# Attention stage: the nine expert parts of two tiles added by four whole additions, in place of one sum along the parts for each tile

## The reference

```
y1  = layernorm(x + attention(x))                    # 4 heads of 32, over 16 sequences at one position
idx = argmax(softmax(y1 @ wg)); gate = the largest probability     # 8 experts, each token goes to one
y   = ((y1 @ w1[idx] + b1[idx]) @ w2[idx] + b2[idx]) # 128 -> 512 -> 128, nothing nonlinear between
out = layernorm(y1 + (gate * y if the token found room at its expert else 0))
```

## Time and profile before

| | |
|---|---|
| median of 3 runs | 4655.11 us (4639.43 to 4656.45) |
| the profiled execution's own time | 4655.05 us |
| its span, first to last instruction | 4653.3 us |
| mean granted TensorE clock | 0.897 |
| busy over the span: PE, DVE, ACT, POOL | 83%, 67%, 37%, 34% |
| attention stage, first to last reduce of the experts | 4083.1 to 4534.6 us |

### The profile page before, as it was taken

How to read it: one execution, slowest core, us unless ns; L and a number is a source line. 1 busy time by engine, 2 the same in 40 slices (tenths; PEclk the granted TensorE clock), 3 DMA queues, 4 the chain that set the end, 5 groups by cost and what they waited for, 6 DMA issues and landing times. The chain is left out here.

```text
span 4653.3 us, 163745 instructions
## 1 busy us (share of the span) xinstructions
PE 3861.4 (83%) x66245; PEld 2812.4 (60%) x66245; DVE 3117.4 (67%) x6104; ACT 1733.8 (37%) x3495; POOL 1595.7 (34%) x2519
## 2 busy tenths in 40 slices
PE   6999999866648998989988989989899998588860
PEld 4666666533326776767776767767677766455530
DVE  3777777747746676767666766767677654288858
ACT  1222222224423343444443433434444432277750
POOL 1333333311004454444444444544444443100001
PEclk6998999988858999999999999999999987699975
DMA  0222222136522222222222222222222221111105
GB/s 25 44 47 46 55 56 49 42 84 155 158 65 49 42 56 41 47 51 48 50 47 49 48 49 40 57 42 47 51 48 49 49 47 26 55 27 28 28 18 149
DMA packets 695281, 251.77 MB, mean 54 GB/s; under 512 B 529368, under 2 KB 660128, under 8 KB 694176
## 3 DMA queue, kind: packets, MB, share of 16 engines
q1 hardware_dynamic: 694560, 241.62, 23.7%
HBM read 154.63 MB, written 86.79 MB: 52 GB/s over the span
## 5 line engine op out<-in xcount | busy, mean ns | idle before, releaser
L1373 POOL TENSOR_TENSOR d_f<-d_ms,d_mhalf 128x16 f32<-128x16 f32 x64 | 239.5, 3742 | 965.1 <-DVE d_ms L1807 965.1
L1567 PE MATMUL d_pa<-d_wv,d_hs 128*128 128x512 f32 x1024 | 517.6, 652 | 0.9 <-DVE d_qk L1778 0.4
L1761 DVE SCALAR_TENSOR_TENSOR d_acc<-d_pa,d_cq,d_acc 128x512 f32<-128x512 f32 x576 | 431.7, 750 | 95.2 <-ACT d_acc L1406 80.3
L1383 POOL TENSOR_TENSOR d_prod<-d_ablk,d_tblk 128x15 f32<-128x15 f32 (+7 forms) x960 | 342.5, 357 | 218.5 <-DMA d_ablk<-a_blocks 147.9
L1387 POOL TENSOR_TENSOR d_tblk<-d_tblk,d_prod 128x28 f32<-128x28 f32 (+7 forms) x896 | 336.4, 375 | 70.8 <-POOL d_prod L1383 0.2
L1567 PEld LDWEIGHTS d_pa<-d_wv,d_hs 128*128 128x128 f32 x1024 | 219.5, 215 | 232.1 <-issue 220.2
L1542 PE MATMUL d_pa<-d_hq,d_wqk 128*128 128x259 f32 x768 | 255.4, 462 | 81.4 <-DVE d_acc L1761 58.0
L1406 ACT ACTIVATE d_acc<-d_pa,d_cq 128x512 f32<-128x512 f32 x192 | 131.9, 687 | 420.8 <-PE d_pa L1542 418.0
L262 POOL TENSOR_TENSOR a_act<-a_act,a_cws 128x512 f32<-128x512 f32 x128 | 166.8, 1316 | 310.2 <-DMA a_cws<-cw_rows 165.3
L1580 PEld LDWEIGHTS d_pb<-d_of_head,d_sqT 128*128 128x128 f32 x2048 | 246.2, 196 | 39.2 <-issue 39.0
L1370 POOL TENSOR_TENSOR d_nr<-d_n,d_half_power 128x16 f32<-128x16 f32 x64 | 188.0, 2938 | 193.8 <-DVE d_n L1846 179.8
(11 more groups left out here) (371 smaller groups left out, 9418.3 us busy)
## 6 DMA issues: line engine op xcount, KB each, us to landing
a_cws<-cw_rows SPq DMA_DIRECT2D x32, 1024.0 KB, 10.5
decays<-g_dec SPq DMA_DIRECT2D x16, 2048.0 KB, 7.3
d_dd<-decays SPq DMA_DIRECT2D x64, 512.0 KB, 4.3
d_hs<-h_t SPq DMA_DIRECT2D x512, 32.0 KB, 2.2
t_blocks<-d_tblk SPq DMA_DIRECT2D x128, 128.0 KB, 1.7
a_blocks<-d_at SPq DMA_DIRECT2D x512, 16.0 KB, 1.9
d_ablk<-a_blocks SPq DMA_DIRECT2D x64, 128.0 KB, 2.1
d_tt<-t_blocks SPq DMA_DIRECT2D x512, 16.0 KB
```

Source lines behind the costliest of these rows:

```text
L1373: pool.tensor_tensor(f[:, :], ms[:, :], mhalf[:, :], ALU.pow).then_inc(sem("f_ready"), 1)
L1383: link(pool.tensor_tensor(prod[:, 0:n, 0:s + 1], ablk[:, s, s + 1:SB].unsqueeze(2).to_broadcast([P, n, s + 1]), tblk[:, 0, s, 0:s + 1].uns ...
L1567: last = pe.matmul(pa[:, B + m, :], hs[:, u % 2, t, :], wv[:, t, cols(m)], start=(t == 0), stop=(t == TAPS - 1))
L1761: last = dve.scalar_tensor_tensor(out=own, in0=raw(e)[:, :, t:t + QT], scalar=cq[:, t, col:col + 1], in1=own, op0=ALU.mult, op1=ALU.add)
```

## The change

`reduce(c)`, called four times in an iteration, becomes `reduce(pair)`, called twice. It takes two tiles by four additions: parts 0 to 3 plus parts 4 to 7 (1024 numbers in each partition), of these the first two plus the second two (512), the first plus the bias part (256), and the last two into `moe` (256). The first three write back into `part`, and each has a `link`. The first pair stands where `reduce(1)` stood, and the second where `reduce(3)` stood. Those who wait for `reduced` count two in an iteration instead of four, and the loop counts 50 links instead of 38.

```diff
@@ sync and scalar: SP before it stores moe, ACT before weigh(0)
-                    hold(sem("reduced"), NC * (i - 1))
+                    hold(sem("reduced"), 2 * (i - 1))
...
-                    wait(act, sem("reduced"), NC * (i - 2))
+                    wait(act, sem("reduced"), 2 * (i - 2))
@@ vector
-                def reduce(c):
+                def reduce(pair):
                     if not main:
                         return
-                    if c == 0:
+                    these = slice(2 * pair, 2 * pair + 2)
+                    if pair == 0:
                         wait(dve, sem("moe_stored"), 16 * NC * (i - 2))
                         dve.wait_ge(sem("bias_taken"), i - 1)
-                    dve.wait_ge(sem("weighed"), HALVES * (i - 2) + 2 * c + 2)
-                    dve.tensor_reduce(moe[:, c, :], part[:, c, :, :].rearrange("p e d -> p d e"), AX_X, ALU.add)\
+                    dve.wait_ge(sem("weighed"), HALVES * (i - 2) + 4 * pair + 4)
+                    link(dve.tensor_tensor(part[:, these, 0:4, :], part[:, these, 0:4, :], part[:, these, 4:8, :], ALU.add))
+                    link(dve.tensor_tensor(part[:, these, 0:2, :], part[:, these, 0:2, :], part[:, these, 2:4, :], ALU.add))
+                    link(dve.tensor_tensor(part[:, these, 0, :], part[:, these, 0, :], part[:, these, NE, :], ALU.add))
+                    dve.tensor_tensor(moe[:, these, :], part[:, these, 0, :], part[:, these, 1, :], ALU.add)\
                        .then_inc(sem("reduced"), 1)
...
-                reduce(0)                    # was behind the sums of the layernorm of y
...
-                reduce(1)
+                reduce(0)                    # behind the sums of the next x
...
-                reduce(2)                    # was behind rden
...
-                reduce(3)
+                reduce(1)                    # ahead of v
```

More of the change, by code:

```diff
@@ L1920, in attention_phase @@
     LOOP_FIRST, LOOP_LAST = 2, 6
-    DVE_LINKS = 38
+    DVE_LINKS = 50
     with ExitStack() as ctx:
```

## The result

| | before | changed |
|---|---|---|
| median of 20 runs each, us | 4640.99 (4629.76 to 4660.17) | 4658.59 (4635.73 to 4672.94) |
| ratio, 95% interval | | 1.0033 [1.0019, 1.0048] |
| profiled execution, us | 4655.05 | 4661.11 |

A forecast was written before the change was run, and what follows sets the result against it. The prediction took a path through `rt`, ACT and PE, not DVE, to bound the attention stage. Delays of 5.2, 0.8, 0.3 and 0.8 us made 7.1 us on 4655.05, forecast 4662 us, range 4641 to 4677.

The forecast's parts named there:

- What bounds the stage: Attention stage: from `rt` to the logits the path is PE and ACT alone, though DVE is busiest at 86%.
- the ring: One attention iteration, 28.5 us: `rt` on DVE, ACT and PE work to the logits, `lm`, routing chain, next `rt`.
- The prices of the additions: The four additions of a pair take 1.22, 0.69, 0.42 and 0.42 us; DVE's busy time falls 48 us.
- The first pair hidden: Additions for tiles 0 and 1, behind the sums of x: hidden by waits for PE, cost and gain nothing.
- The second pair: Additions for tiles 2 and 3 behind the last `weigh`: `lm` 3.40 us after their start instead of 2.97, 0.43 later.
- The sum, 7.1 us: Delay over all iterations: 12 x 0.43 = 5.2 us, plus 0.8, 0.3 and 0.8 in iterations 15, 16 and 17.
- iteration 4's 0.70 us wait of `v`: First iteration in the loop: `v` had waited 0.70 us for PE, which takes the whole delay, so 0.
- its allowance for dearer additions: Upper bound 4677 us: an extra 1.0 us, one held-up addition, in each of 15 iterations.
- a DVE bound: Rival, 5%: DVE sets the pace of the attention stage; 2.7 us saved an iteration, 43 us in all, 4612 us.
- The free tail: Rival, 15%: the 0.43 us ahead of `lm` is swallowed; only the last iterations' 1.9 us stay, 4657 us.
- Additions held up by POOL: Rival, 5%: two additions behind the last `weigh` held up 0.95 us each, 28 us more in 15 iterations, 4690 us.

The follow-up runs named there:

- first pair only: Kernel before with tiles 0 and 1 added by four additions, tiles 2 and 3 still summed where they were: ratio 1.0011 [0.9992, 1.0030].
- last tile alone: Changed kernel with tile 2 added earlier, behind `rden`, and only tile 3 added ahead of `v`: ratio to the kernel before 1.0003 [0.9985, 1.0020].

## Why the prediction was right, and where it was short

- *What bounds the stage*: right. Not the busiest engine, but the ring over `rt`, ACT and PE; taking 1.3 and 2.2 us of each iteration off DVE gained nothing (first pair only, last tile alone).
- *The prices of the additions*: 1.23, 0.69, 0.43, 0.43 against 1.22, 0.69, 0.42, 0.42, and 49 us less of DVE's work against 48. The rows that the prices came from are products of the same sizes (L1868, L523); the additions took the same within 0.02 us.
- *The first pair hidden*: right. `h` is in time and `on` waits for PE, 3.3 us in iteration 4 where 3 were expected.
- *The second pair*: right to 0.01 us, 3.39 against 3.40, and 28.85 in an iteration against 28.9.
- *The sum, 7.1 us*: this step was too small, less than half of the 15 us measured. As the ring's own share it nearly holds: 5.6 us over iterations 2 to 14 against 5.2; behind them stand 4.0 against 1.9, with a lower clock in that stretch too (0.82 and 0.73 in the last two iterations against 0.99 and 0.61). What is missing is that the granted clock would change with the ring's length: 17.7 us of the stage in the profiled execution. I took iteration 4's 0.70 us wait of `v` for the start of the loop; it was a fall of the clock (the mean granted clock of that iteration is 0.85), the only one there, and its 33.11 us against 28.42 said what another one costs. The sum put the clock at nothing without a reason. That the median, 4658.59, came so near to 4662 is luck: the 7.1 us stood on a median of three runs that lay 14 us above that of twenty, and on 4641 they give 4648, 10.5 too low. As a ratio, 1.0015 was forecast and 1.0033 measured; the range reached so far by its allowance for dearer additions, 1.0 us in each iteration, which did not come.
- *The rivals*: a DVE bound was refuted, and came true only where three copies more were put on DVE. The free tail was refuted. Additions held up by POOL: not seen, here not even in the first pair, which was to stretch by 1.0 us; in six of thirteen iterations it was POOL that waited, below.

## What to carry to other kernels

Look for what the wait in front of an instruction leaves behind it: batching two tiles halves the instructions but puts both tiles' work behind the last one's arrival, so batch what is early and keep alone what comes last. Time saved on an engine off the ring is worth nothing until work of the ring is moved onto it; here three copies turned it into 0.5%, where the same copies on the kernel with the sums gave 0.26%. And where PE works in bursts, price a longer ring also by the granted clock, iteration by iteration.

## What was not expected of the hardware

- A delay of 0.43 us in each iteration of 28.4 raised the falls of TensorE's clock to 1.2 GHz from one to four whole ones (4.3 us each) and three or four part ones (1.4 us), alike in three kernels, one execution each; 1.04 us gave a part fall in every iteration but the first, and iterations of 27.0 to 28.1 us had no whole one. Before the fall shown above PE had worked in bursts, 1.0 to 1.4 of each 2 us, but it did the same in iterations without a fall. What picks the iteration is open.
- The first pair's first addition and POOL's power of 1.01 us start within 0.2 us of each other. By the exclusion that the earlier trace rows show and the Trainium skill states ("SBUF — State Buffer", section "Who interferes with whom"), one of the two should wait for the other. Which one does, and whether, hangs here on which came first. In iteration 6 POOL was first, by 0.03 us, and neither waited; in iteration 7 the addition was first, by 0.08 us, and POOL's power took 2.02 us:

```profile
4189.16 1.01 POOL L2075 TENSOR_TENSOR e_rstd<-e_ve,e_mhalf 128x4 f32<-128x4 f32 x1 [5.10 <-DVE e_ve L2345]
4189.19 1.25 DVE L2375 TENSOR_TENSOR e_part<-e_part 128x1024 f32<-128x1024 f32 x1
...
4221.76 1.23 DVE L2375 TENSOR_TENSOR e_part<-e_part 128x1024 f32<-128x1024 f32 x1
4221.84 2.02 POOL L2075 TENSOR_TENSOR e_rstd<-e_ve,e_mhalf 128x4 f32<-128x4 f32 x1 [5.10 <-DVE e_ve L2345]
```

  In iterations 2 to 14 the addition was first six times, and POOL's power took 1.92 to 2.08 us in each; in the other seven it took 1.01, and the addition at most 1.25. In the kernels whose first two tiles are summed the power always took 1.01 us in the stage. So an addition in progress holds POOL up, as the Trainium skill says, while a POOL operation on 4 numbers did not hold DVE up, as the one on 512 in the earlier trace rows did. The stretched power is hidden: h comes only behind the whole pair.
